# Attention column sums: the R matmuls in another place of TensorE's queue, and every second block's sums taken on ScalarE

## The chip, the cores and the metric

The kernel is one program on all 8 cores of one Trainium2 chip. Each core works on its own 4096 tokens and its own heads; nothing is exchanged between cores. The metric is the device time in microseconds of the slowest core, from one launch. The profile shows one execution, by its slowest core, core 2.

## The reference

One layer: attention and a feed-forward part with eight low-rank experts, each with layer norms and a residual. Only the attention's middle matters here:

```python
Q = Q.reshape(N, heads, L, dh)      # K and V the same; plain reshape
scores = jnp.einsum('neax,nebx->neab', Q * scale, K * scale)
A = jax.nn.softmax(scores, axis=2)              # over a, the query index
Out = jnp.einsum('neab,neax->neax', A, V)       # A is summed over b
```

The softmax runs over `a`, and the second product only sums `A` over `b`. So with e = exp(scores) two vectors are wanted for each head: the column sums c[b], the sum of e[a,b] over a, and r[a], the sum of e[a,b] / c[b] over b. `Out` is then V times r. With L = 8192 and dh = 64, a core has eight heads and computes 8192 x 8192 exponentials for each.

## The kernel before

The program has four blocks in order. Block A makes the layer norm and Q, K and V; Q and K stay in SBUF as `qt` and `kt`, two heads to a tile of 128 partitions, four pairs of heads. Block B computes r. Block C applies it and the output projection, block D is the feed-forward part. Every engine has its own queue, written out by hand; semaphores tie the queues together. The change touches block B alone.

Block B runs over K = 0 to 255: `p = K // 64` is the pair of heads, `k` the chunk of 128 key positions b. One K is called a step here. A step has these parts:

- **Fills**, TensorE L421 and L427. For each of eight pairs of slots (`s2`), four matmuls 64x512 write scores of 1024 query positions for head A and for head B, the two heads in the two halves of the array at once. `ps_sl` has three slots of 128x1024 in PSUM. The fill of one pair waits for the head-A exponential of the pair before it (`s_exp >= gsB - 2`).
- **Exponentials**, ScalarE L463, or L455 where `K % 8 == 0`: sixteen of 128x1024, head A and head B by turns, from PSUM into `eA` and `eB` (bf16, two buffers each, by the parity of K). L455 also gives the sum of each row (`accum_out`, eight partial sums into `caA`, `caB`). Before step K ScalarE waits for R(K-2) (`s_rmm`), which frees the buffer, and for lhsTall of K-2 (`s_lhs`).
- **Column sums**, VectorE. After the last exponential of K, it adds the eight partial sums (L479, L481) where `K % 8 == 0`; else it scans `eA` and `eB`, 128x8192 each, with a running sum (L484, L488). Then two reciprocals, a memset, and two small writes (L497, L500) put 1/c into `lhsTall`; the second one sets `s_lhs`.
- **R(K)**, TensorE L390 and L397, function `emit_R`: sixteen pairs of matmuls 128x512 with a stationary operand of 16 columns, of which one holds 1/c; they add this step's share of r into the bank `rps`, head A in partitions 0 to 15, head B in 32 to 47. R(K) needs all exponentials of K and `s_lhs` of K. At the end of a pair of heads (`K % 64 == 63`) VectorE waits for R(K) and copies `rps` out.

The order on TensorE is: first fill of K, R(K-2), the other seven fills of K; after the last step R(254) and R(255).

Of the kernel before, what the change touches and what calls it, by code (L numbers as in the profile page):

```python
# [22 lines left out]
NK = 256  # L23
# [6 lines left out]
def build_program():  # L30
# [48 lines left out]
    with ExitStack() as top:  # L79
# [53 lines left out]
        with ExitStack() as scqt:  # L133
# [215 lines left out]
            with ExitStack() as sc2:  # L349
# [26 lines left out]
                @blockB.tensor  # L376
                def _(tensor):
                    if "B" not in DBG_PHASES:
                        return
                    def emit_R(Kr):  # L380
                        if Kr < 0:
                            return
                        p, k = Kr // 64, Kr % 64
                        par = Kr % 2
                        W(tensor, "s_exp", (Kr + 1) * 16)
                        W(tensor, "s_lhs", Kr + 1)
                        if k == 0:
                            W(tensor, "s_rev", p)
                        for j in range(16):
                            mm = tensor.matmul(  # L390
                                rps[0:16, :], lhsT_ap(par, j, 0),
                                eA[:, par, j * 512:(j + 1) * 512],
                                start=(k == 0 and j == 0),
                                stop=(k == 63 and j == 15),
                                skip_group_check=True,
                                tile_position=(0, 0))
                            mm = tensor.matmul(  # L397
                                rps[32:48, :], lhsT_ap(par, j, 1),
                                eB[:, par, j * 512:(j + 1) * 512],
                                start=(k == 0 and j == 0),  # L400
                                stop=(k == 63 and j == 15),
                                skip_group_check=True,
                                tile_position=(0, 32))
                        I(mm, "s_rmm")

                    for K in range(NK):
                        p, k = K // 64, K % 64
                        for s2 in range(8):
                            if s2 == 1:
                                emit_R(K - 2)  # L410
                            gsA = K * 16 + 2 * s2
                            gsB = gsA + 1
                            slA = gsA % 3
                            slB = gsB % 3
                            W(tensor, "s_exp", gsB - 2)
                            lhsA = kt[0:64, p, k * 128:(k + 1) * 128]
                            lhsB = kt[64:128, p, k * 128:(k + 1) * 128]
                            mms = []
                            for half in range(2):
                                a0 = s2 * 1024 + half * 512  # L420
                                mms.append(tensor.matmul(  # L421
                                    ps_sl[:, slA,
                                          half * 512:(half + 1) * 512],
                                    lhsA, qt[0:64, p, a0:a0 + 512],
                                    start=True, stop=True,
                                    tile_position=(0, 0)))
                                mms.append(tensor.matmul(  # L427
                                    ps_sl[:, slB,
                                          half * 512:(half + 1) * 512],
                                    lhsB, qt[64:128, p, a0:a0 + 512],  # L430
                                    start=True, stop=True,
                                    tile_position=(64, 0)))
                            I(mms[2], "s_fill")
                            I(mms[3], "s_fill")
                    emit_R(NK - 2)
                    emit_R(NK - 1)

                @blockB.scalar
                def _(scalar):
                    if "B" not in DBG_PHASES:  # L440
                        return
                    for K in range(NK):
                        par = K % 2
                        W(scalar, "s_rmm", K - 1)
                        W(scalar, "s_lhs", K - 1)
                        for s in range(16):
                            gs = K * 16 + s
                            head = s % 2
                            s2 = s // 2
                            sl = gs % 3  # L450
                            W(scalar, "s_fill", gs + 1)
                            ebuf = eA if head == 0 else eB
                            cab = caA if head == 0 else caB
                            if K % 8 == 0:
                                I(scalar.activation(  # L455
                                    ebuf[:, par, s2 * 1024:(s2 + 1) * 1024],
                                    ps_sl[:, sl, :], AF.Exp,
                                    scale=float(2.0 ** -10),
                                    bias=epsb[:, 1:2],
                                    accum_out=cab[:, par, s2:s2 + 1]),  # L460
                                  "s_exp")
                            else:
                                I(scalar.activation(  # L463
                                    ebuf[:, par, s2 * 1024:(s2 + 1) * 1024],
                                    ps_sl[:, sl, :], AF.Exp,
                                    scale=float(2.0 ** -10),
                                    bias=epsb[:, 1:2]), "s_exp")

                @blockB.vector
                def _(vector):  # L470
                    if "B" not in DBG_PHASES:
                        return
                    for K in range(NK):
                        par = K % 2
                        W(vector, "s_exp", (K + 1) * 16)
                        W(vector, "s_rmm", K - 1)
                        v0 = cnt["s_dv"]
                        if K % 8 == 0:
                            I(vector.reduce_sum(cA[:, 0:1], caA[:, par, :],  # L479
                                                axis=AX.X), "s_dv")  # L480
                            I(vector.reduce_sum(cB[:, 0:1], caB[:, par, :],  # L481
                                                axis=AX.X), "s_dv")
                        else:
                            I(vector.tensor_scalar(  # L484
                                eA[:, par, :], eA[:, par, :],
                                1.0, 0.0, ALU.mult, ALU.add,
                                accum_out=cA[:, 0:1]), "s_dv")
                            I(vector.tensor_scalar(  # L488
                                eB[:, par, :], eB[:, par, :],
                                1.0, 0.0, ALU.mult, ALU.add,  # L490
                                accum_out=cB[:, 0:1]), "s_dv")
                        vector.wait_ge(sem("s_dv"), v0 + 2)
                        I(vector.reciprocal(icA[:, 0:1], cA[:, 0:1]), "s_dv")
                        I(vector.reciprocal(icB[:, 0:1], cB[:, 0:1]), "s_dv")
                        I(vector.memset(lhsTall[:, par, :], 0.0), "s_dv")
                        vector.wait_ge(sem("s_dv"), v0 + 5)
                        I(vector.tensor_scalar(lhsT_write_ap(par, 0),  # L497
                                               ones16[:, :], icA[:, 0:1],
                                               None, ALU.mult), "s_dv")
                        I(vector.tensor_scalar(lhsT_write_ap(par, 1),  # L500
                                               ones16[:, :], icB[:, 0:1],
                                               None, ALU.mult), "s_lhs")
                        if K % 64 == 63:
                            pp = K // 64
                            W(vector, "s_rmm", K + 1)
                            I(vector.tensor_scalar(
                                r_ev[0:16, pp * 512:(pp + 1) * 512],
                                rps[0:16, :], -1.0, None, ALU.add), "s_dv")
                            I(vector.tensor_scalar(
                                r_od[0:16, pp * 512:(pp + 1) * 512],  # L510
                                rps[32:48, :], -1.0, None, ALU.add),
                              "s_rev")
# [715 lines left out]
```

How the kernel before makes its waits and increments, by code:

```python
        def W(eng, name, v):  # L107
            if v > 0:
                eng.wait_ge(sem(name), v)
# [1 line left out]
        def I(instr, name, k=1):  # L111
            instr.then_inc(sem(name), k)
            cnt[name] += k
# [47 lines left out]
                @blockA.sync  # L161
                def _(sync):
                    for dst, src in [
                        (bq[:, :], bq_d), (bk[:, :], bk_d), (bv[:, :], bv_d),
                        (bo[:, :], bo_d), (wib[:, :], wib_d),
                        (wob[:, :], wob_d), (gb[:, :], gb_d),
                        (identf8[:, :], ident_d[0:8, 0:8]),
                        (epsb[:, :], epsc_d),
                    ]:
                        I(sync.dma_start(dst, src), "sA", 16)
                    if "A" not in DBG_PHASES:
                        sync.wait_ge(sem("sA"), cnt["sA"])
                        return
                    for gi in range(NCH):
                        W(sync, "s_xfree", gi - 1)
                        I(sync.dma_start(xb[:, gi % 2, :],
                                         x_d[gi * 128:(gi + 1) * 128, :]),
                          "sX%d" % (gi % 2), 16)
# [1 line left out]
                @blockA.gpsimd  # L180
# [15 lines left out]
                    ]  # L196
                    assert len(loads) == N_GPRE
                    for dst, src in loads:
                        I(gpsimd.dma_start(dst, src), "sG", 16)
                    if "A" not in DBG_PHASES:
                        gpsimd.wait_ge(sem("sG"), cnt["sG"])
                        return
                    for e in range(NB):
```

## Time and the profile before

| | us |
|---|---|
| median of 3 runs | 9051.24 (9051.23 to 9086.05) |
| the profiled execution's own time | 9053.95 |
| its span on core 2 | 9052.4 |
| spans of the 8 cores | 9029.4 to 9052.4 |
| TensorE matmuls busy | 5074.8 |
| VectorE busy | 5402.6 |
| ScalarE busy | 4396.9 |
| block B, first to last exponential on core 2 | 658.9 to 6764.7 |

The span runs from the first to the last instruction of the core; the execution's time is a little longer. Busy times are sums over instructions of an engine. Block B has two thirds of the span. The granted TensorE clock has two levels, 1.2 and 2.4 GHz; the records give it as 0.5 and 1.0, and its mean over core 2 is 0.687.

### The profile page before, as it was taken

Reading aid. Unit: us, or ns where it says so; the run is one execution under the profiler, and the core shown is the slowest. Engines: PE = TensorE matmul, PEld = TensorE weight load, DVE = VectorE, ACT = ScalarE, POOL = GpSimd, SP = SyncE. Lnnn points to the kernel's source line nnn. Section 1 sums busy time; section 2 is a strip of 40 time slices with the busy share of each in tenths; the row PEclk is TensorE's granted clock in tenths of the full one; section 3 lists DMA queues with packets and bytes.
Section 4 is the critical chain, followed back from the end, with each engine's and each line's share of the span. In section 5 each row is a group of like instructions: output and inputs, shape, how many; then the busy total and the mean of one; then the engine's idle time right before and its main releaser. Section 6 shows DMA issues by size and latency. Waiting matters only on the chain. (4 is left out here: it accounts for less than half of the span.)

```text
span 9052.4 us, 69885 instructions; the slowest of 8 cores (9029.4 to 9052.4 us)
## 1 busy us (share of the span) xinstructions
PE 5074.8 (56%) x24072; PEld 1527.3 (17%) x24072; DVE 5402.6 (60%) x4272; ACT 4396.9 (49%) x4868; POOL 151.2 (2%) x144
## 2 busy tenths in 40 slices
PE   4665555555555555555555555555552336677776
PEld 2221111111111111111111111111111112233322
DVE  4656676767676666767676766676764663322223
ACT  0017677777767676767676777777660000000000
POOL 0000000000000000000000000000000000000000
PEclk8776666666666666666666666666665667888888
DMA  3100000000000000000000000000004224644565
GB/s 71 42 28 0 1 1 1 0 1 0 1 1 0 1 1 0 1 1 0 1 1 0 1 1 0 1 1 0 1 0 106 69 78 65 92 62 61 72 77 75
DMA packets 348262, 206.26 MB, mean 23 GB/s; under 512 B 303840, under 2 KB 320224, under 8 KB 346864
## 3 DMA queue, kind: packets, MB, share of 16 engines
q0 software_dynamic: 273920, 92.70, 9.1%
q1 hardware_dynamic: 74000, 109.10, 4.1%
q8 instruction: 202, 3.31, 0.2%
q14 instruction: 140, 1.15, 0.0%
HBM read 235.75 MB, written 50.33 MB: 32 GB/s over the span
## 5 line engine op out<-in xcount | busy, mean ns | idle before, releaser
L421 PE MATMUL ps_sl<-qt,kt 64*128 64x512 bf16 x4096 | 1850.2, 547 | 2831.4 <-ACT eA L463 2443.1
L484 DVE TENSOR_SCALAR_CACHE_REDUCE eA<-eA 128x8192 bf16<-128x8192 bf16 x224 | 1945.7, 8686 | 1658.0 <-ACT eB L463 1658.0
L463 ACT ACTIVATE eA<-ps_sl,epsb 128x1024 bf16<-128x1024 f32 x1792 | 1998.7, 1115 | 1569.9 <-PE rps L397 1293.8
L463 ACT ACTIVATE eB<-ps_sl,epsb 128x1024 bf16<-128x1024 f32 x1792 | 1992.4, 1112 | 0.0
L488 DVE TENSOR_SCALAR_CACHE_REDUCE eB<-eB 128x8192 bf16<-128x8192 bf16 x224 | 1944.5, 8681 | 0.0
L427 PE MATMUL ps_sl<-qt,kt 64*128 64x512 bf16 x4096 | 1894.9, 559 | 0.0
L390 PE MATMUL rps<-eA,lhsTall 128*16 128x512 bf16 x4096 | 1407.5, 520 | 16.2 <-DVE lhsTall L500 16.2
L397 PE MATMUL rps<-eB,lhsTall 128*16 128x512 bf16 x4096 | 1407.3, 520 | 0.0
L421 PEld LDWEIGHTS ps_sl<-qt,kt 64*128 64x128 bf16 x4096 | 274.6, 98 | 4315.2 <-issue 4315.2
L1057 ACT ACTIVATE s4lv<-s4vr,epsb 128x1 f32<-128x1 f32 x32 | 9.4, 294 | 1324.8 <-DVE s4vr L1141 1324.8
L390 PEld LDWEIGHTS rps<-eA,lhsTall 128*16 128x16 bf16 x4096 | 451.0, 115 | 1039.5 <-issue 895.7
L1029 PE MATMUL ps_wi<-interT,wotb 128*128 128x512 bf16 x2048 | 498.3, 409 | 135.3 <-DMA wotb<-wot 125.6
L1012 PE MATMUL ps_wi<-h2t,wit_s 128*128 128x512 bf16 x2048 | 494.9, 385 | 14.0 <-DVE mxr L1101 14.0
L397 PEld LDWEIGHTS rps<-eB,lhsTall 128*16 128x16 bf16 x4096 | 453.1, 116 | 0.0
L1109 DVE TENSOR_SCALAR interT<-ps_wi,wib_s 128x512 bf16<-128x512 f32 x256 | 192.2, 751 | 375.9 <-PE ps_wi L1017 375.9
L1117 DVE TENSOR_SCALAR ft_sb<-ps_wi,wob_s 128x512 bf16<-128x512 f32 x64 | 48.1, 751 | 585.9 <-PE ps_wi L1029 585.9
L455 ACT ACTIVATE eA<-ps_sl,epsb 128x1024 bf16<-128x1024 f32 x256 | 285.2, 1114 | 208.9 <-PE rps L397 184.0
L455 ACT ACTIVATE eB<-ps_sl,epsb 128x1024 bf16<-128x1024 f32 x256 | 284.0, 1109 | 0.0
L1029 PEld LDWEIGHTS ps_wi<-interT,wotb 128*128 128x128 bf16 x2048 | 210.2, 104 | 421.7 <-issue 217.5
L297 ACT ACTIVATE st_lv<-st_vr,epsb 128x1 f32<-128x1 f32 x32 | 9.4, 294 | 553.0 <-DVE st_vr L239 553.0
L700 PE MATMUL ps_h<-identb,h2b 128*128 128x128 bf16 x256 | 32.4, 305 | 396.7 <-DVE h2b L826 396.7
L427 PEld LDWEIGHTS ps_sl<-qt,kt 64*128 64x128 bf16 x4096 | 253.1, 104 | 0.0
(123 smaller groups left out, 3036.9 us busy)
## 6 DMA issues: line engine op xcount, KB each, us to landing
wotb<-wot POOLq DMA_DIRECT2D x64, 1024.0 KB, 11.2
xb<-x SPq DMA_DIRECT2D x64, 512.0 KB, 4.0
x1buf<-x1b SPq DMA_DIRECT2D x32, 512.0 KB, 5.0
x1b<-x1buf SPq DMA_DIRECT2D x32, 512.0 KB, 4.2
y<-yb SPq DMA_DIRECT2D x32, 512.0 KB, 5.0
vsp<-vt_tmp POOLq DMA_DIRECT2D x64, 128.0 KB, 2.2
vt<-vsp SPq DMA_DIRECT2D x8, 1024.0 KB, 6.1
wit_s<-wit POOLq DMA_DIRECT2D x1, 8192.0 KB, 69.1
```

The costliest lines, as they stand in the source:

```text
L390: mm = tensor.matmul(rps[0:16, :], lhsT_ap(par, j, 0), eA[:, par, j * 512:(j + 1) * 512], start=(k == 0 and j == 0), stop=(k == 63 and j = ...
L397: mm = tensor.matmul(rps[32:48, :], lhsT_ap(par, j, 1), eB[:, par, j * 512:(j + 1) * 512], start=(k == 0 and j == 0), stop=(k == 63 and j ...
L421: mms.append(tensor.matmul(ps_sl[:, slA, half * 512:(half + 1) * 512], lhsA, qt[0:64, p, a0:a0 + 512], start=True, stop=True, tile_positio ...
L427: mms.append(tensor.matmul(ps_sl[:, slB, half * 512:(half + 1) * 512], lhsB, qt[64:128, p, a0:a0 + 512], start=True, stop=True, tile_posit ...
L455: I(scalar.activation(ebuf[:, par, s2 * 1024:(s2 + 1) * 1024], ps_sl[:, sl, :], AF.Exp, scale=float(2.0 ** -10), bias=epsb[:, 1:2], accum_ ...
L463: I(scalar.activation(ebuf[:, par, s2 * 1024:(s2 + 1) * 1024], ps_sl[:, sl, :], AF.Exp, scale=float(2.0 ** -10), bias=epsb[:, 1:2]), "s_exp")
L484: I(vector.tensor_scalar(eA[:, par, :], eA[:, par, :], 1.0, 0.0, ALU.mult, ALU.add, accum_out=cA[:, 0:1]), "s_dv")
L488: I(vector.tensor_scalar(eB[:, par, :], eB[:, par, :], 1.0, 0.0, ALU.mult, ALU.add, accum_out=cB[:, 0:1]), "s_dv")
L1012: tensor.matmul(ps_wi[:, fc % 2, :], wit[:, ci, fc * 128:(fc + 1) * 128], h2t4[:, par, ci, :], start=(ci == 0), stop=False)
L1029: mm = tensor.matmul(ps_wi[:, co % 2, :], wotb[:, co % 2, fc, :], interT[:, fc, :], start=(fc == 0), stop=(fc == FC - 1))
L1109: I(vector.tensor_scalar(interT[:, fc, :], ps_wi[:, fc % 2, :], wib[:, fc:fc + 1], 0.0, ALU.add, ALU.max), "s4_ie")
L1117: I(vector.tensor_scalar(ft_sb[:, e % 2, co, :], ps_wi[:, co % 2, :], wob[:, co:co + 1], None, ALU.add), "s4_fe")
```

## The change

The R matmuls change place: `emit_R(K - 1)` stands behind all eight fills of K, where before `emit_R(K - 2)` stood behind the first fill of K. The condition for row sums on ScalarE becomes `K % 2 == 0` on both engines, so that VectorE scans only the odd steps. The flag `skip_group_check=True` of the R matmuls goes. Waits, buffers and semaphores stay as they are; their values follow the calls.

```diff
--- before.py
+++ after.py
@@ -392,22 +392,18 @@
                                 eA[:, par, j * 512:(j + 1) * 512],
                                 start=(k == 0 and j == 0),
                                 stop=(k == 63 and j == 15),
-                                skip_group_check=True,
                                 tile_position=(0, 0))
                             mm = tensor.matmul(
                                 rps[32:48, :], lhsT_ap(par, j, 1),
                                 eB[:, par, j * 512:(j + 1) * 512],
                                 start=(k == 0 and j == 0),
                                 stop=(k == 63 and j == 15),
-                                skip_group_check=True,
                                 tile_position=(0, 32))
                         I(mm, "s_rmm")
 
                     for K in range(NK):
                         p, k = K // 64, K % 64
                         for s2 in range(8):
-                            if s2 == 1:
-                                emit_R(K - 2)
                             gsA = K * 16 + 2 * s2
                             gsB = gsA + 1
                             slA = gsA % 3
@@ -432,7 +428,7 @@
                                     tile_position=(64, 0)))
                             I(mms[2], "s_fill")
                             I(mms[3], "s_fill")
-                    emit_R(NK - 2)
+                        emit_R(K - 1)
                     emit_R(NK - 1)
 
                 @blockB.scalar
@@ -451,7 +447,7 @@
                             W(scalar, "s_fill", gs + 1)
                             ebuf = eA if head == 0 else eB
                             cab = caA if head == 0 else caB
-                            if K % 8 == 0:
+                            if K % 2 == 0:
                                 I(scalar.activation(
                                     ebuf[:, par, s2 * 1024:(s2 + 1) * 1024],
                                     ps_sl[:, sl, :], AF.Exp,
@@ -475,7 +471,7 @@
                         W(vector, "s_exp", (K + 1) * 16)
                         W(vector, "s_rmm", K - 1)
                         v0 = cnt["s_dv"]
-                        if K % 8 == 0:
+                        if K % 2 == 0:
                             I(vector.reduce_sum(cA[:, 0:1], caA[:, par, :],
                                                 axis=AX.X), "s_dv")
                             I(vector.reduce_sum(cB[:, 0:1], caB[:, par, :],
```

## Rows read from the trace of the kernel before

**Rows 1.** The page's 40 equal slices: busy tenths of ScalarE, TensorE's clock in tenths.
```profile
ACT  0017677777767676767676777777660000000000
...
PEclk8776666666666666666666666666665667888888
```

**Rows 2.** The page's groups: busy us, mean ns of one; idle before, releaser.
```profile
L463 ACT ACTIVATE eA<-ps_sl,epsb 128x1024 bf16<-128x1024 f32 x1792 | 1998.7, 1115 | 1569.9 <-PE rps L397 1293.8
...
L455 ACT ACTIVATE eA<-ps_sl,epsb 128x1024 bf16<-128x1024 f32 x256 | 285.2, 1114 | 208.9 <-PE rps L397 184.0
```

**Rows 3.** Times of L463: ns, first and last start; idle before it, times.
```profile
L463 ACT ACTIVATE eA<-ps_sl,epsb x1792: 1113/1113/1132, 678.5 to 6763.7; 128x1024 bf16<-128x1024 f32 x200
...
  PE rps L397: 1293.8, 223
```

**Rows 4.** Timeline of one plain step, K = 99: start us, duration us.
```profile
3014.87 0.59 PE L390 MATMUL rps<-eA,lhsTall 128*16 128x512 bf16 x1
...
3019.99 0.38 PE L390 MATMUL rps<-eA,lhsTall 128*16 128x512 bf16 x1
...
3020.59 1.11 ACT L463 ACTIVATE eA<-ps_sl,epsb 128x1024 bf16<-128x1024 f32 x1 [5.83 <-PE rps L397]
...
3021.84 0.37 PE L421 MATMUL ps_sl<-qt,kt 64*128 64x512 bf16 x1 [1.47 <-ACT eA L463]
...
3022.06 0.37 PE L421 MATMUL ps_sl<-qt,kt 64*128 64x512 bf16 x1
...
3024.59 1.13 ACT L463 ACTIVATE eA<-ps_sl,epsb 128x1024 bf16<-128x1024 f32 x1
...
3026.97 1.11 ACT L463 ACTIVATE eA<-ps_sl,epsb 128x1024 bf16<-128x1024 f32 x1 [0.25 <-PE ps_sl L427]
...
3036.42 1.11 ACT L463 ACTIVATE eA<-ps_sl,epsb 128x1024 bf16<-128x1024 f32 x1 [0.24 <-PE ps_sl L427]
3037.43 1.11 ACT L463 ACTIVATE eB<-ps_sl,epsb 128x1024 bf16<-128x1024 f32 x1
```

**Rows 5.** Timeline of VectorE there: the sums of K = 98.
```profile
3014.95 8.69 DVE L484 TENSOR_SCALAR_CACHE_REDUCE eA<-eA 128x8192 bf16<-128x8192 bf16 x1 [4.99 <-ACT eB L463]
...
3033.36 0.26 DVE L500 TENSOR_SCALAR lhsTall<-ones_s,icB 128x16 bf16<-128x16 bf16 x1
```

**Rows 6.** Two windows of it: busy us (times) by engine; PEclk is the clock.
```profile
3014.86:3018.72 3.86, 3.86 (x22) 1.30 (x22) 3.77 (x1) 0.00 (x0) 0.00 (x0) 0.50 0.00 0
3018.72:3025.55 6.83, 2.87 (x24) 0.82 (x20) 6.83 (x3) 4.96 (x5) 0.00 (x0) 1.00 0.00 0
```

**Rows 7.** Timeline at the end of block B: R(254) and R(255).
```profile
6762.94 0.63 PE L421 MATMUL ps_sl<-qt,kt 64*128 64x512 bf16 x1
...
6763.53 0.59 PE L390 MATMUL rps<-eA,lhsTall 128*16 128x512 bf16 x1
...
6763.67 1.11 ACT L463 ACTIVATE eA<-ps_sl,epsb 128x1024 bf16<-128x1024 f32 x1 [0.24 <-PE ps_sl L427]
...
6768.25 0.38 PE L390 MATMUL rps<-eA,lhsTall 128*16 128x512 bf16 x1
...
6784.80 0.59 PE L390 MATMUL rps<-eA,lhsTall 128*16 128x512 bf16 x1 [16.17 <-DVE lhsTall L500]
...
6790.80 0.38 PE L390 MATMUL rps<-eA,lhsTall 128*16 128x512 bf16 x1
```

**Rows 8.** Timeline of ScalarE in one summing step, K = 96.
```profile
2948.80 1.11 ACT L455 ACTIVATE eA<-ps_sl,epsb 128x1024 bf16<-128x1024 f32 x1 [5.93 <-PE rps L397]
2949.81 0.19 ACT L455 ACTIVATION_READ_ACCUMULATOR eA<-ps_sl,epsb 128x1 f32 x1
...
2953.16 1.12 ACT L455 ACTIVATE eA<-ps_sl,epsb 128x1024 bf16<-128x1024 f32 x1
...
2955.63 1.11 ACT L455 ACTIVATE eA<-ps_sl,epsb 128x1024 bf16<-128x1024 f32 x1 [0.15 <-PE ps_sl L427]
...
2965.44 1.11 ACT L455 ACTIVATE eA<-ps_sl,epsb 128x1024 bf16<-128x1024 f32 x1 [0.15 <-PE ps_sl L427]
```

## The prediction

> **What bounds the kernel now.** I read the page's slices first, then the times of one line, then the order of events in single steps of block B. The slices [rows 1] show block B as the long flat middle, from the third to the 31st of 40 slices, with ScalarE at six or seven tenths and a granted clock of TensorE between its levels. The page's groups [rows 2] say what fills it: exponentials of 128x1024 at about 1.115 us each, 3584 on L463 and 512 on L455. The times of L463 [rows 3] give the length of a step. The first head-A exponential of K = 1 starts at 678.5 and that of the last pair of K = 255 at 6763.7. Inside one step the same distance (first to last pair) is 3036.42 - 3020.59 = 15.83 us [rows 4], so 254 steps take 6085.2 - 15.8 = 6069.4 us, 23.895 us each. Of this ScalarE stands idle waiting for the last R matmul (L397) 223 times, 1293.8 us, 5.8 us each time [rows 3].
>
> The order of events in a step [rows 4] says why. R(K-2) starts at 3014.87, its sixteenth pair of matmuls at 3019.99, and ScalarE, idle for 5.83 us, starts at 3020.59. R stands behind the first fill on TensorE, the first fill waits for the last head-A exponential of the step before, and ScalarE may not begin step K before R(K-2) has freed the exponentials' buffer. So R lies entirely on the path. After it the eight pairs go at 2.00 us while the clock is at 2.4 GHz (20.59 to 24.59, two pairs) and at 2.36 us when it is at 1.2 GHz (26.97 to 36.42, four pairs): at the low clock a fill is longer than the head-B exponential beside it, and ScalarE loses 0.24 us a pair. VectorE's two scans are not the limit: they start at 3014.95 and the last write of lhsTall starts at 3033.36 [rows 5], well before the step's end.
>
> **The clock.** TensorE is at 1.2 GHz when R starts and stays there for 3.86 us with 22 matmuls back to back (the last two of the fill and ten pairs of R, so 0.42 us from one pair to the next), and at 2.4 GHz for the next 6.83 us [rows 6]; then, with a short fill every 2 us, it is low again for the rest of the step. R buys the fast clock for its own second half and for two fills.
>
> **Part 1, R(K-1) behind all fills of K, instead of R(K-2) behind its first one.** R(0) to R(253) are moved; matmuls and weight loads stay the same in number. The new order stands once in this trace, at the end of block B, where R(254) already follows the fills of K = 255 [rows 7]. The last fill's third matmul starts at 6762.94, R at 6763.53, and the last head-A exponential at 6763.67, so R runs beside the last two exponentials. I write down the distance from the start of that exponential (A7) to the first one of the next step (A0). R starts 0.14 before A7 [rows 7]. First to last of its pairs is 5.12 [rows 4]. Then comes the first fill of the next step; its slot is free, since its wait is for A7. The step from R's last pair to it shows nowhere in this order: at least 0.22, the spacing of matmuls at the fast clock (3021.84 to 3022.06, [rows 4]), and at most 0.59, the opposite change at the low clock (6762.94 to 6763.53, [rows 7]). I take 0.30, near the low end, because the clock is high there. From the fill's first matmul to A0: 0.22 to its third, which lasts 0.37 [rows 4], and 0.10 of handoff, as from the third's end at 6763.57 to 6763.67 [rows 7]: 0.69. Sum: -0.14 + 5.12 + 0.30 + 0.69 = 5.97 us.
>
> In the kernel before, this distance is 23.895 less the mean first-to-last distance. That is 15.83 for a plain step and, for a step with the sums on ScalarE (which I call a summing step), 2965.44 - 2948.80 = 16.64 [rows 8]; one in eight: 15.93. So 7.96, and the move saves 1.99 us a step. It isn't the whole 5.8: A7 and B7 hide 2.1 of R, the old first fill was hidden and the new one's 0.69 is not.
>
> The weight change at that step has a rule. The Trainium skill, "TensorE: Matmul & The Clock Gate", section "The mechanism" under packing, says that a weight load overlaps running matmuls only where their row groups differ. R uses all 128 rows, so by the rule a fill's load of about 0.1 us would stand bare behind it and the step would be some 0.32, 5 us more in all. No row here shows that step; the sum doesn't use it.
>
> **Part 2, sums on ScalarE in every second K instead of every eighth.** The summing steps among K = 1 to 254 rise from 31 to 127, by 96. Each exponential there is followed by an accumulator read of about 0.2 us [rows 8]. It costs less than its sixteen reads, because at the low clock it lies in the 0.24 us that ScalarE would wait for the fill. Two of its pairs take 2.18 us at the fast clock and the others 2.46 [rows 8]. First to last pair is 16.64 against 15.83, 0.81 a step: 96 x 0.81 = 78 us slower. VectorE loses two scans of 8.69 us in 96 steps, about 1670 us of its work. That is worth nothing by itself, as it was hidden, but it gives the cover that part 1 needs. R(K-1) now waits for lhsTall of K-1 at the end of K instead of one fill into K+1. After a plain K-1 (always odd) it is ready 3033.36 + 0.26 - 3014.76 = 18.9 us after the end of its last exponential, where 3014.76 is A0's start less its idle time [rows 4, 5]. R wants it after the new gap, 5.97 - 2.12 = 3.85 (2.12 from A7's start to B7's end: 3036.42, 3037.43 + 1.11), and the seven pairs of a summing K, 16.64, less 0.14: at 20.35 us. So 1.4 us of slack. Were K plain too, 0.6 would be left; if it fell short, the fills queued behind R on TensorE would be late, and ScalarE with them. After a summing K-1 the wait is for a few small instructions.
>
> **Part 3, the dropped group-check flag**: no instruction's shape or count comes from it; nothing.
>
> **Sum.** Plain step 15.83 + 5.97 = 21.80; summing step 16.64 + 5.97 = 22.61; 127 of each: mean 22.205 against 23.895, 1.69 x 254 = 429 us less. By parts: 254 x 1.99 - 78 = 427. The first step, the last R and the other blocks are unchanged. The profiled execution, 9053.95 (span 9052.4), would become 8624.7; against the median of the runs, 9051.24, it is 8622.
>
> **The rivals.** *The clock rises later or earlier in R.* The step isn't as even as before: plain and summing steps differ by 0.8 us, so R meets the clock's rise elsewhere. Three R of this trace differ in just this: first to last pair 5.12 in the step shown, 4.72 for R(254), 6.00 for R(255) [rows 4, 7]. Later: +0.88 x 254 = +224, 8846 us. Earlier: -0.40 x 254 = -102, 8520. The clock then also ends earlier or later against the fills, one pair of 0.36 us the other way, so both are outer values. The page on TensorE named above says, under "What's actually happening", that the place of the rise changes from run to run; the three R agree that it isn't fixed.
>
> *Slower: the clock doesn't rise at all.* The fills alone never raise it in the low part of a step. If R's run were broken up, R would take 15 times 0.42 = 6.3 us (1.2 more), the bare fill 1.11 in place of 0.69 (0.42 more; from its third matmul's start it is 0.73 at the low clock, 6762.94 to 6763.67, and 0.38 lies ahead of that), and the two fast pairs 0.36 or, with sums, 0.28 more each (2.46 less 2.18, [rows 8]; 0.64 in the mean): 2.3 us a step, 580 us, 9202 in all. It decides from 1.69 us a step. For it: the change makes the busy stretch depend on lhsTall. Against: R now has a fill directly ahead and one directly behind, and R(254) in that place got the fast clock [rows 7]. The same page's table "Why this matters for your kernels" warns that pauses between bursts bring the low clock; that stays true of the fills here, before and after.
>
> *The move gives nothing,* because ScalarE waits for the fill behind R as it waited for R; then only the reads count: 9051 + 78 = 9129. R(254), with A7 starting 0.14 us into it [rows 7], speaks against it.
>
> *R waits for lhsTall.* Each us beyond the slack costs 127 us; 1 us gives 8749. The slack of 1.4 us speaks against it.
>
> **How the numbers follow.** Forecast 0.75; clock later 0.12; clock earlier 0.05; R waits 0.03; clock never 0.03; nothing from the move 0.02. The time is the forecast's, 8622. Its own bounds, the step of 0.22 to 0.59, give 8602 to 8696. With the earlier clock below, and a part of the later one and a short wait above, the range is 8515 to 8740. Half a per cent, 45 us, is about what a measurement of this kernel can tell from no change. Faster 0.94, same 0.01, slower 0.05.
>
> **What would show it.** In the profile after: the distance between first exponentials of two neighbouring steps sums to about 44.4 us; ScalarE's idle time before A0 is about 3.85 us and put down to the fill's matmul, not R's; A7 starts within 0.2 us of R's start; no idle time of TensorE before R for VectorE; 1024 accumulator reads a head instead of 256; 128 scans a head instead of 224; R first to last near 5.1. Wrong would be: R of 6 us in most steps, an idle time before R, or pairs of more than 2.46 us in summing steps.

## The result and the profile after

The changed kernel takes 8623.7 us in the median of eight executions, against 8622 forecast. The kernel before, run beside it, took 9070.4; the ratio is 0.951, with a 95% interval of 0.949 to 0.953. In some executions the cores of one die or of both show a lower granted clock and take some per cent longer, so times given here as medians are of the other executions, only one of which is left of e9_split_sums_warm, and the profile of e7_changed_warm is of such a longer one. The profiled execution took 8629.9 us, its slowest core 7. These are lines of its page, which answer to [rows 1] and [rows 2]. The groups give busy us, mean ns of one, and the idle time before it with what ended it.

```profile
DVE  4663444444444444444444444444436653322233
ACT  0007777777777777777777787777730000000000
...
PEclk8886666666666666666666666666665658988877
...
L480 DVE TENSOR_SCALAR_CACHE_REDUCE eA<-eA 128x8192 bf16<-128x8192 bf16 x128 | 1111.8, 8686 | 2456.6 <-ACT eB L459 2456.6
...
L451 ACT ACTIVATE eA<-ps_sl,epsb 128x1024 bf16<-128x1024 f32 x1024 | 1142.2, 1115 | 671.0 <-PE ps_sl L423 658.6
L459 ACT ACTIVATE eA<-ps_sl,epsb 128x1024 bf16<-128x1024 f32 x1024 | 1143.1, 1116 | 530.0 <-PE ps_sl L423 530.0
```

VectorE's scans are 128 for head A and as many for head B, where they were 224 each; one takes 8.69 us as in [rows 5]. The releaser of ScalarE's idle time has changed: before it was R (L397), now it is the matmul of a fill (L423 is the fill's head B here). The exponentials themselves take 1.115 us as before.

The times of L459 on core 7 (columns as in [rows 3]) give the length of a step: 6330.6 - 679.3 less 15.83, over 254, is 22.187 us. The forecast was 22.205, before it was 23.895.

```profile
L459 ACT ACTIVATE eA<-ps_sl,epsb x1024: 1114/1114/1132, 679.3 to 6330.6; 128x1024 bf16<-128x1024 f32 x171
...
  PE ps_sl L423: 530.0, 770
```

The first of two neighbouring transitions on core 7, timeline: R behind the last fill of a plain step, the last head-A exponential A7, R's last pair, the first fill of the next step, A0.

```profile
3002.49 0.59 PE L390 MATMUL rps<-eA,lhsTall 128*16 128x512 bf16 x1
...
3002.63 1.11 ACT L459 ACTIVATE eA<-ps_sl,epsb 128x1024 bf16<-128x1024 f32 x1 [0.24 <-PE ps_sl L423]
...
3008.25 0.38 PE L390 MATMUL rps<-eA,lhsTall 128*16 128x512 bf16 x1
...
3008.57 0.39 PE L417 MATMUL ps_sl<-qt,kt 64*128 64x512 bf16 x1
...
3009.27 1.11 ACT L451 ACTIVATE eA<-ps_sl,epsb 128x1024 bf16<-128x1024 f32 x1 [4.52 <-PE ps_sl L423]
```

This is the sum of the prediction, term by term, in one transition: R 0.14 ahead of A7, R's first to last pair 5.76 (5.12 was taken), from there to the fill 0.32 (0.30), from the fill to A0 0.70 (0.69). ScalarE's idle time is 4.52, forecast 3.85. The next transition on the same core, behind a summing step:

```profile
3025.79 0.59 PE L390 MATMUL rps<-eA,lhsTall 128*16 128x512 bf16 x1
...
3025.92 1.11 ACT L451 ACTIVATE eA<-ps_sl,epsb 128x1024 bf16<-128x1024 f32 x1 [0.15 <-PE ps_sl L423]
...
3030.15 0.38 PE L390 MATMUL rps<-eA,lhsTall 128*16 128x512 bf16 x1
...
3030.47 0.39 PE L417 MATMUL ps_sl<-qt,kt 64*128 64x512 bf16 x1
...
3031.17 1.11 ACT L459 ACTIVATE eA<-ps_sl,epsb 128x1024 bf16<-128x1024 f32 x1 [2.94 <-PE ps_sl L423]
```

Here R takes 4.36 and the idle time is 2.94; the step from R to the fill is again 0.32. From A7 to A0 it is 5.25 in one and 6.64 in the other, 5.95 in the mean (5.97 forecast). A third pair of rows from the same core shows that this goes on by turns:

```profile
3047.00 1.11 ACT L459 ACTIVATE eA<-ps_sl,epsb 128x1024 bf16<-128x1024 f32 x1 [0.24 <-PE ps_sl L423]
...
3053.64 1.11 ACT L451 ACTIVATE eA<-ps_sl,epsb 128x1024 bf16<-128x1024 f32 x1 [4.52 <-PE ps_sl L423]
```

Core 2, same execution, has the other pattern: the long transition comes behind the summing step.

```profile
3005.06 1.11 ACT L451 ACTIVATE eA<-ps_sl,epsb 128x1024 bf16<-128x1024 f32 x1 [3.39 <-PE ps_sl L423]
...
3021.71 1.11 ACT L451 ACTIVATE eA<-ps_sl,epsb 128x1024 bf16<-128x1024 f32 x1 [0.15 <-PE ps_sl L423]
...
3028.08 1.11 ACT L459 ACTIVATE eA<-ps_sl,epsb 128x1024 bf16<-128x1024 f32 x1 [4.07 <-PE ps_sl L423]
```

Its idle times are 3.39 and 4.07; the step shown is 23.02 us, and the one behind it 21.36, 44.38 together. On core 7 the two make 44.37 (3009.27 to 3053.64). Cores 6 and 7 have the first pattern and cores 0 to 5 the second. So no core has the even transition of the prediction; its mean is there, 5.91 to 5.95 us on all eight.

The granted clock over two steps of core 7, in windows cut where it changes (busy us and times by engine; the clock is the number after POOL):

```profile
3007.62:3014.45 6.83, 2.77 (x22) 0.67 (x18) 6.83 (x3) 5.18 (x9) 0.00 (x0) 1.00 0.00 0
3014.45:3028.10 13.65, 7.43 (x32) 1.63 (x34) 8.89 (x7) 12.89 (x24) 0.00 (x0) 0.50 0.00 1
3028.10:3034.93 6.83, 4.07 (x34) 1.24 (x30) 1.34 (x7) 3.89 (x6) 0.00 (x0) 1.00 0.00 0
3034.93:3052.00 17.07, 10.37 (x48) 2.54 (x48) 2.69 (x1) 12.97 (x13) 0.00 (x0) 0.50 0.00 1
```

One high stretch of 6.83 us belongs to each step, as before. The low stretch behind it was 17.07 us in the kernel before; here it is 13.65 and 17.07 by turns.

### The profile page after: what moved, and what is told of

Read it like the earlier page. It is cut to its first block and busy times, and to the rows that moved or that the text cites. A ratio compares the mean times of both kernels' runs of the same rounds, so it can differ in the third digit from the quotient of the medians.

```text
span 8628.3 us, 71229 instructions; the slowest of 8 cores (8600.0 to 8628.3 us)
## 1 busy us (share of the span) xinstructions
PE 4962.3 (58%) x24072; PEld 1517.7 (18%) x24072; DVE 3764.3 (44%) x4080; ACT 4540.8 (53%) x6404; POOL 151.2 (2%) x144
## 5 line engine op out<-in xcount | busy, mean ns | idle before, releaser
L417 PE MATMUL ps_sl<-qt,kt 64*128 64x512 bf16 x4096 | 1746.7, 519 | 2539.8 <-ACT eA L451 1318.0
L480 DVE TENSOR_SCALAR_CACHE_REDUCE eA<-eA 128x8192 bf16<-128x8192 bf16 x128 | 1111.8, 8686 | 2456.6 <-ACT eB L459 2456.6
L423 PE MATMUL ps_sl<-qt,kt 64*128 64x512 bf16 x4096 | 1786.1, 530 | 0.0
L459 ACT ACTIVATE eA<-ps_sl,epsb 128x1024 bf16<-128x1024 f32 x1024 | 1143.1, 1116 | 530.0 <-PE ps_sl L423 530.0
L390 PE MATMUL rps<-eA,lhsTall 128*16 128x512 bf16 x4096 | 1393.2, 516 | 15.1 <-DVE lhsTall L496 15.1
L459 ACT ACTIVATE eB<-ps_sl,epsb 128x1024 bf16<-128x1024 f32 x1024 | 1139.9, 1113 | 0.0
L484 DVE TENSOR_SCALAR_CACHE_REDUCE eB<-eB 128x8192 bf16<-128x8192 bf16 x128 | 1111.1, 8681 | 0.0
L417 PEld LDWEIGHTS ps_sl<-qt,kt 64*128 64x128 bf16 x4096 | 267.4, 97 | 3909.0 <-issue 3909.0
L475 DVE TENSOR_REDUCE cA<-caA 128x1 f32<-128x8 f32 x128 | 20.5, 160 | 622.1 <-ACT eB L451 622.1
```

The source lines that it names most:

```text
L390: mm = tensor.matmul(rps[0:16, :], lhsT_ap(par, j, 0), eA[:, par, j * 512:(j + 1) * 512], start=(k == 0 and j == 0), stop=(k == 63 and j = ...
L417: mms.append(tensor.matmul(ps_sl[:, slA, half * 512:(half + 1) * 512], lhsA, qt[0:64, p, a0:a0 + 512], start=True, stop=True, tile_positio ...
L423: mms.append(tensor.matmul(ps_sl[:, slB, half * 512:(half + 1) * 512], lhsB, qt[64:128, p, a0:a0 + 512], start=True, stop=True, tile_posit ...
L459: I(scalar.activation(ebuf[:, par, s2 * 1024:(s2 + 1) * 1024], ps_sl[:, sl, :], AF.Exp, scale=float(2.0 ** -10), bias=epsb[:, 1:2]), "s_exp")
L480: I(vector.tensor_scalar(eA[:, par, :], eA[:, par, :], 1.0, 0.0, ALU.mult, ALU.add, accum_out=cA[:, 0:1]), "s_dv")
L484: I(vector.tensor_scalar(eB[:, par, :], eB[:, par, :], 1.0, 0.0, ALU.mult, ALU.add, accum_out=cB[:, 0:1]), "s_dv")
```

## The experiments

**Part 1 alone (e1_move_only)**: both conditions back to one step in eight.

```diff
-if K % 2 == 0:      # exponentials and column sums
+if K % 8 == 0:
```

> Part 1 alone: R(K-1) behind the fills of K as in the changed kernel, sums on ScalarE where K % 8 == 0 as before. Theory A (the step is the sum of its parts): plain steps 21.80 us, 31 summing steps 22.61, mean 21.90 against 23.895, 507 us less than before, some 8545 (78 below the changed kernel), and the 0.6 us of slack of R against the scan is just enough. Theory B (the steps fall into step with the clock's rises and falls, so that a step's length is set by where R meets the rise): steps of unequal length from about 20.9 to 22.6, mean near 21.76, some 8510. Rival C (R waits for lhsTall after two plain steps and the fills behind it are late): an idle time of TensorE before R put down to VectorE, and at 1 us or more in most steps the gain over the changed kernel is gone.

Measured: 8515.7 us in the median, ratio 0.941 (0.934 to 0.949). This is 108 us less than the changed kernel. The two weren't run side by side, but the steps say the same: 22.187 less 21.76, times 254, is 108 us. Core 0, who waited for lhsTall (total us, times), and the exponentials' first and last start:

```profile
L390 PE MATMUL rps<-eA,lhsTall x4096: 379/417/634, 705.8 to 6259.2; 128*16 128x512 bf16 x196
...
  DVE lhsTall L496: 30.1, 65
```

```profile
L459 ACT ACTIVATE eA<-ps_sl,epsb x1792: 1114/1114/1133, 689.4 to 6232.1; 128x1024 bf16<-128x1024 f32 x200
```

The step is (6232.1 - 689.4 - 15.83) / 254 = 21.76 us; theory B said 21.76, theory A 21.90. R does wait for VectorE, in 64 steps besides the last R (whose 16.2 us are the scan itself), but 30.1 - 16.2 = 13.9 us over 64 waits is 0.2 us each. Rival C is out at this size. Steps of 20.92, 21.37 and 22.58 us stand side by side. The clock's low stretch is 13.65 us in 158 of the steps and 17.07 in the others.

**Part 2 alone (e2_sums_only)**: the kernel before with the sums of every second step on ScalarE.

```diff
-if K % 8 == 0:
+if K % 2 == 0:
```

> Part 2 alone: R(K-2) behind the first fill of K as before, sums on ScalarE where K % 2 == 0. Theory A: the reads cost 0.81 us in each of 96 more steps, 78 us, so 0.9% slower than before. Theory B: a summing step is longer and the plain one behind it shorter by the same, the two together as long as the high and the low stretch of the clock in two steps (2 x 23.9), so within 0.1% of before. VectorE's lower load changes nothing in either.

Measured: 9053.8 us in the median, beside 9057.9 of the kernel before; ratio 0.998 (0.995 to 1.001). 96 more summing steps cost nothing that can be seen. A0 of three neighbouring steps on core 0:

```profile
3020.26 1.11 ACT L463 ACTIVATE eA<-ps_sl,epsb 128x1024 bf16<-128x1024 f32 x1 [5.25 <-PE rps L397]
...
3043.85 1.11 ACT L455 ACTIVATE eA<-ps_sl,epsb 128x1024 bf16<-128x1024 f32 x1 [5.63 <-PE rps L397]
...
3068.05 1.11 ACT L463 ACTIVATE eA<-ps_sl,epsb 128x1024 bf16<-128x1024 f32 x1 [5.25 <-PE rps L397]
```

The plain step is 23.59 and the summing one 24.20, together 47.79: two high and two low stretches of the clock, 2 x (6.83 + 17.07) = 47.80, which is what the clock's records of this core show in all steps but one. The kernel before has the same stretches (the high one of 6.83 us is in [rows 6]) and its mean step is as long as the two. The reads do lengthen the pairs: the mean distance from A0 to A7 is 16.25 us, where it was 15.94. But R's first to last pair is 4.78 in the mean, where it was 5.12, because R meets the rise of the clock sooner, and so the step stays as it was. This is theory B. The 78 us of the prediction are there in the pairs and are given back by R.

**All sums on ScalarE in the changed order (e3_all_sums)**

```diff
-if K % 2 == 0:
+if True:
```

> The changed kernel with the sums on ScalarE in every step, no scan on VectorE at all. Theory A: every step 22.61 us, 254 x 0.405 = 103 us slower than the changed kernel, some 8725. Theory B: mean near 22.53, some 8710, steps unequal. If lhsTall were what holds R anywhere in the changed kernel, this one would be faster than it.

Measured: 8691.6 us, ratio 0.958 (0.953 to 0.963); the mean step is 22.52 on core 2, with steps from 21.7 to 23.3. That is B's mean; it is 18 us below B's total and 33 below A's. The changed kernel isn't held by lhsTall anywhere: its TensorE waits for lhsTall once, before the last R (15.1 us on core 7), and taking the scan away altogether makes it 68 us slower.

**No sums on ScalarE (e4_no_sums)**

```diff
-if K % 2 == 0:
+if K < 0:
```

> The changed order of R with no sums on ScalarE at all: VectorE scans every step. It takes away the cover of part 2 to the last. Theory A: plain steps of 21.80 us and 0.6 us of slack left for the scan, so 254 x 0.405 = 103 us less than the changed kernel, some 8520. Theory B (settling with the clock): steps of about 20.9, 21.4 and 22.6 by turns, mean near 21.63, some 8480; TensorE waits some 0.4 us for lhsTall before an R in the shorter ones and this costs nothing, because a later R meets the rise of the clock sooner. Rival C: the wait for lhsTall falls on the steps, mean above 22.2, and the sums on ScalarE were needed.

Measured: 8522.8 us in the median (8495.3 the lowest), ratio 0.938 (0.932 to 0.944). Core 4, waits for lhsTall and the exponentials' first and last start (K = 0 included):

```profile
  DVE lhsTall L496: 47.8, 88
```

```profile
L459 ACT ACTIVATE eA<-ps_sl,epsb x2048: 1114/1115/1135, 658.3 to 6204.6; 128x1024 bf16<-128x1024 f32 x187
```

(6204.6 - 658.3 - 15.86) / 255 = 21.69 us a step, near B's 21.63 and 0.11 below A. The 87 waits before the last are 31.6 us, 0.36 each. Against e1_move_only (21.75 over the same steps, its first included) they cost nothing that can be seen; a late R meets the clock's rise sooner (4.80 us in the mean from its first to its last pair). At the three borders between pairs of heads a step takes 26.3 us, because VectorE copies `rps` out before it can begin the next scan. In e1_move_only, with a summing step there, none is above 23.1, so the borders eat up part of what this one would have gained on it.

**The clock held high in both orders (e8_all_sums_warm, e10_before_all_sums_warm)**: three matmuls whose result nobody reads stand behind each of seven fills, so TensorE has work in every pair. All sums are on ScalarE in both, so only R's place differs. The added matmuls change no output.

```diff
+dps = e2(nc.psum_tensor("dps", [128, 512], F32))
...
 I(mms[3], "s_fill")
+for _d in range([3, 3, 3, 3, 3, 3, 3, 0][s2]):
+    tensor.matmul(dps[:, :], kt[:, p, k * 128:(k + 1) * 128],
+                  qt[:, p, 0:512], start=True, stop=True)
```

(In e10_before_all_sums_warm the list is `[0, 3, 3, 3, 3, 3, 3, 3]` and R is `emit_R(K - 2)` behind the first fill.)

> e3_all_sums (sums on ScalarE in every step) with the same added matmuls as e7_changed_warm. No scan, so no wait for VectorE: every step 7 x 2.18 + 4.0 = 19.3 us against 22.52 of e3_all_sums, 820 us less than it, some 7870. If e7_changed_warm shows the wait for lhsTall, this one is faster than it by some 100 us, although without the added matmuls all sums on ScalarE were slower.

> The order of before, R(K-2) behind the first fill, with the sums on ScalarE in every step and three matmuls that nobody reads behind the fills 1 to 7, so that the clock stays high: the counterpart of e8_all_sums_warm (step 19.30), with only the place of R different. It measures the move without the clock. First to last pair 15.3; then the fill waits 1.45 for A7 and its sum, takes 0.5, R 3.2 and the handoff 0.6: 5.8, step 21.1. So the move is worth 1.8 us a step at a steady clock, against 1.99 in the sum of the prediction; some 8320 in all.

Measured, one execution each: 7864.9 us and 8346.2 us. ScalarE's first and last start and its idle time, core 0, first e8_all_sums_warm:

```profile
L456 ACT ACTIVATE eA<-ps_sl,epsb x2048: 1112/1154/1272, 657.9 to 5593.5; 128x1024 bf16<-128x1024 f32 x187
...
  PE ps_sl L424: 479.8, 257
```

Then e10_before_all_sums_warm:

```profile
L460 ACT ACTIVATE eA<-ps_sl,epsb x2048: 1112/1141/1265, 658.5 to 6069.7; 128x1024 bf16<-128x1024 f32 x187
...
  PE rps L398: 870.0, 254
  PE ps_sl L428: 70.3, 62
```

Between A0 of K = 0 and A7 of K = 255 stand 255 steps and 15.3 us: 19.3 us a step in the one and 21.2 in the other. Both sums of parts, 19.3 and 21.1, hold to 0.1 us once the clock is nearly still: it is at 2.4 GHz for over 99% of block B in the one and for 96 to 97% in the other, and R's first to last pair is 3.24 us in both, in every step of core 0. Moving R is worth 1.9 us a step there, 481 us in all, of which 460 are idle time of ScalarE before head-A exponentials (870.0 + 70.3 less 479.8). From A7 to A0 alone it is 1.77 us; the rest is in the pairs, from the short low stretches that only e10_before_all_sums_warm has.

**The changed kernel with the clock held high (e7_changed_warm)**: the same added matmuls in the changed kernel.

> The changed kernel with three matmuls that nobody reads behind each of the fills 0 to 6, so that the clock stays high. It takes the clock out of the step: ScalarE's first to last pair falls to 7 x 2.00 = 14.0 in a plain step and 7 x 2.18 = 15.3 in a summing one, R to 15 x 0.215 = 3.2, and the distance from A7 to the next A0 to some 4.0. Then the scan is no longer covered: lhsTall of a plain K-1 is ready 18.9 us after its last exponential, R wants it after 1.9 + 15.3 - 0.2 = 17.0. Expected: plain step 18.0, summing step 19.3 + 2 of waiting for VectorE, mean 19.7, 630 us less than the changed kernel, some 7990, with an idle time of TensorE of about 2 us before every second R. If the clock isn't what sets the step's length, it stays near 22.2.

Measured: 8181 us in the median, 8179 in the lowest, ratio 0.905 (0.895 to 0.915); 191 us above the forecast. The wait for VectorE came, and it came with something else. The profiled execution took 8330.7 us, but its excess lies behind block B (2427 to 2439 us on cores 2 to 5, 2271 to 2281 on the others). In block B the mean step is 20.46 to 20.48 us on all eight cores, against 19.7 forecast, and 255 times this difference is the 191 us and a little more. Core 3, end of a summing step behind a plain one:

```profile
4027.86 1.20 ACT L456 ACTIVATE eA<-ps_sl,epsb 128x1024 bf16<-128x1024 f32 x1
...
4029.68 0.59 PE L391 MATMUL rps<-eA,lhsTall 128*16 128x512 bf16 x1 [1.97 <-DVE lhsTall L501]
...
4032.61 0.38 PE L391 MATMUL rps<-eA,lhsTall 128*16 128x512 bf16 x1
...
4034.34 0.38 PE L391 MATMUL rps<-eA,lhsTall 128*16 128x512 bf16 x1
...
4035.36 1.11 ACT L464 ACTIVATE eA<-ps_sl,epsb 128x1024 bf16<-128x1024 f32 x1 [5.11 <-PE ps_sl L424]
```

Three windows over it (busy us and times by engine; the clock is the number after POOL):

```profile
4024.00:4029.20 5.20, 2.05 (x12) 0.50 (x11) 4.93 (x6) 5.20 (x11) 0.00 (x0) 1.00 0.00 2
4029.20:4032.60 3.40, 2.92 (x14) 1.01 (x16) 1.68 (x9) 1.05 (x2) 0.00 (x0) 0.50 0.03 5
4032.60:4036.00 3.40, 3.40 (x27) 1.09 (x23) 0.00 (x0) 0.64 (x1) 0.00 (x0) 1.00 0.00 0
```

TensorE stands idle for 1.97 us before R, and R finds the clock at 1.2 GHz, which it keeps for 3.4 us; it takes 4.66 instead of 3.2, and the step is 22.8 instead of the 21.3 forecast (the plain one is 18.1, forecast 18.0). What I had not priced is the clock's fall in the idle time. The same execution shows a third level of the clock in other stretches, core 0, one window of 200 us:

```profile
3000.00:3200.00 200.00, 160.06 (x840) 42.97 (x839) 94.92 (x79) 166.31 (x235) 0.00 (x0) 0.81 0.00 1
```

Here it is granted at 0.81, and matmuls of R follow at 0.26 us instead of 0.22. This level has 47% of block B on core 0 and 13% on core 3, and the mean step is the same on both; so in block B of this kernel it costs nothing that can be seen. Behind block B it does: cores 2 to 5 have it there for 1200 us or more, the others not at all.

**R spread over the fills (e5_spread)**: sums on ScalarE in every step, and R(K-1) cut into pieces behind the fills 1 to 7 of K.

```diff
+RC = [0, 0, 3, 6, 8, 10, 12, 14, 16]     # first pair of R behind each fill
...
 I(mms[3], "s_fill")
-emit_R(K - 1)                            # behind all fills
+emit_R(K - 1, RC[s2], RC[s2 + 1])        # pairs j0 to j1 - 1; the waits at
+                                         # j0 == 0, s_rmm at j1 == 16
```

> A version meant to be better. Sums on ScalarE in every step, so that 1/c of K-1 is ready about 2 us after the last exponential of K-1; the sixteen pairs of R(K-1) are spread behind the fills 1 to 7 of K, as 3, 3, 2, 2, 2, 2, 2. TensorE is idle for 1.4 us in every pair of slots and two pairs of R take 0.85 at the low clock, so R leaves the path, if the weight changes between fill and R cost no more than some 0.2 us each way. Expected: a step of eight pairs at 2.46 us if the clock stays low, 19.7, some 8000 in all; at 2.18 us if it stays high, 17.5, some 7440. If fills wait for R instead: a pair of slots above 2.5 us and little gain over the changed kernel.

Measured: 7667.5 us, ratio 0.844 (0.839 to 0.849). Core 6, low clock: three pairs of R, one fill, the next piece of R.

```profile
3009.94 0.59 PE L391 MATMUL rps<-eA,lhsTall 128*16 128x512 bf16 x1
...
3010.08 1.11 ACT L454 ACTIVATE eA<-ps_sl,epsb 128x1024 bf16<-128x1024 f32 x1 [0.15 <-PE ps_sl L426]
...
3010.76 0.63 PE L391 MATMUL rps<-eA,lhsTall 128*16 128x512 bf16 x1
...
3011.43 0.58 PE L420 MATMUL ps_sl<-qt,kt 64*128 64x512 bf16 x1
...
3012.39 0.59 PE L391 MATMUL rps<-eA,lhsTall 128*16 128x512 bf16 x1
...
3012.53 1.11 ACT L454 ACTIVATE eA<-ps_sl,epsb 128x1024 bf16<-128x1024 f32 x1 [0.15 <-PE ps_sl L426]
```

The next head-A exponential comes 2.45 us after the last, as in a summing step without R between its fills [rows 8] (2.46 there): R costs nothing. The page:

```profile
ACT  0005999999999999999999999999100000000000
...
PEclk9787777777777777777777777777665588888888
```

ScalarE is busy in nine tenths, and the step is 18.48 us, between the two bounds 17.5 and 19.7, since the clock is high for about half of the time. Against e3_all_sums, with the same sums, the step is 4.0 us shorter. Even with the clock low throughout it would be 2.8 shorter (22.52 less the 19.7 of the expectation, an estimate); the rest comes with the clock, which is high for 54% of block B here and for 30% there.

**The same with the clock held high (e6_spread_warm)**: one to four added matmuls behind each fill, by `[4, 1, 1, 2, 2, 2, 2, 2]`.

> e5_spread with matmuls added that nobody reads (128x512 into a spare bank: 4 behind fill 0, 1 behind fills 1 and 2, 2 behind the others), so that TensorE is busy for about 1.2 us of every 2.2 in all of block B and the clock, once it is at 2.4 GHz, has no cause to fall. In e5_spread a step was 18.48 us in the mean with pairs of 2.18 and 2.46 us mixed. Theory B (what is left is the clock): all pairs 2.18, step 17.45, 255 x 1.03 = 260 us less than e5_spread, some 7400. If the added matmuls get in the way of the fills instead, the step is longer than 18.5.

Measured: 7509.8 us, ratio 0.828 (0.824 to 0.832). The step is 17.53 us (17.45 forecast), 0.95 less than in e5_spread (242 us in all). The total came out only 158 us lower; the rest lies outside block B, where the code is the same. On the slowest core, 3, the part behind block B took 2368 us, 88 more than on the slowest of e5_spread. The extra time goes with the 0.81 level: cores 2 to 5 have it for some 900 us behind block B and take 2349 to 2368 us there, the others have none of it and take 2261 to 2274. Ahead of block B it is the other way round: cores 0, 1, 6 and 7 have it for 370 to 410 us and take 699 to 706 us, the others 655 to 657. What brings this level on is open.

**Head B's sums in pieces on VectorE (e9_split_sums_warm)**: from e6_spread_warm, with ScalarE's sums for head A only, R behind the fills 2 to 7, and the added matmuls by `[4, 4, 1, 1, 1, 1, 2, 2]`.

```diff
-RC = [0, 0, 3, 6, 8, 10, 12, 14, 16]
+RC = [0, 0, 0, 3, 6, 9, 12, 14, 16]
...
+for c in range(8):
+    W(vector, "s_exp", K * 16 + 2 * c + 2)
+    I(vector.tensor_scalar(eB[:, par, c * 1024:(c + 1) * 1024],
+                           eB[:, par, c * 1024:(c + 1) * 1024],
+                           1.0, 0.0, ALU.mult, ALU.add,
+                           accum_out=caB[:, par, c:c + 1]), "s_dv")
```

> A version meant to be better still, from e6_spread_warm: head B's sums go to VectorE, which adds up each 128x1024 piece while the exponentials run (about 1.1 us each, estimated as an eighth of the scan's 8.69), head A's stay on ScalarE. R(K-1) begins behind fill 2, since 1/c comes some 3 us after the last exponential. ScalarE's pair is 1.10 + 1.005 = 2.10 instead of 2.18, step 16.8: 255 x 0.65 = 160 us less than e6_spread_warm, some 7240. If 1/c comes later than fill 2's end, the fills behind R are late and the gain is smaller.

Measured: 7263.7 us in one execution, 0.80 of the 9051.5 that was the lowest of the kernel before beside it. No interval can be given for it. Its new group on core 5:

```profile
L481 DVE TENSOR_SCALAR_CACHE_REDUCE eB<-eB 128x1024 bf16<-128x1024 bf16 x2048 | 2492.3, 1218 | 1390.4 <-ACT eB L467 1390.0
```

A piece of 128x1024 takes 1.22 us instead of 1.1, which is still covered. The step is 16.8 us in 234 of 255, as forecast, and 16.9 in the mean, since a few take over 20 us. This is the fastest version seen; ScalarE's exponentials alone are 16 x 1.0 us of it.

## Why the prediction was right

- *What bounds the kernel.* Right: R on the path with ScalarE idle, and pairs of 2.00 or 2.36 us by the clock. e5_spread shows it from the other side: with R off the path, and the clock high for longer by it, 4 us a step go.
- *R's new place.* The terms -0.14, 0.30 and 0.69 were measured at -0.14, 0.32 and 0.70. The estimate for the middle one by the Trainium skill ("TensorE: Matmul & The Clock Gate", "The mechanism") was 0.32, since there a weight load overlaps running matmuls only where their row groups differ. The size agrees with the trace; the rule doesn't hold throughout in it. R's own loads share all 128 rows with the matmuls that run, and yet its pairs follow at 0.22 us with a load of 0.09 in between (core 7, 3007.82 to 3008.04). What costs the 0.10 more between R and a fill is not shown.
- *R's own time.* I took 5.12 for every step. Hardly a step has it: 5.76 and 4.36 on core 7, with a mean of 5.06. The rivals "clock later" and "clock earlier" are both there, by turns, and cancel. My bounds for them, 6.00 and 4.72, were taken as alternatives to each other, which they aren't, and 4.36 lies below the lower one. This is the weak step of the prediction: R was a constant, but the runs show its mean at 5.12, 4.78, 4.85 or 5.06 us, by what else stands in the step.
- *The two parts.* Both were mis-sized, through R, and against each other. The move alone was put at 505 us (254 x 1.99) and is worth 542 (9057.9 less 8515.7). The sums were put at 78 us; they cost 108 in the new order (8623.7 less 8515.7) and 0 in the old one. The 0.81 us of a summing step isn't what was wrong: from A0 to A7 the sums add 0.29 to 0.31 us to the mean step in both orders, 74 to 79 us in all (table below). The rest is R. In the new order it is 0.21 us longer with the sums (against that, the waits of e1_move_only, 0.07 in the mean, are gone), in the old order 0.34 shorter. That the two errors, 37 and 30 us, cancel in the total is luck.
- *The cover that the sums would give.* It wasn't needed. I had put the slack at 0.6 us with plain steps on both sides; the runs show R late by 0.2 to 0.4 us in some steps, because a short step comes sooner than the mean one, and no loss by it. A wait costs time only once the rest is faster: in e7_changed_warm it is near 2 us and costs more than itself, since the clock falls in it.
- *The dropped flag.* Matmuls and weight loads are 24072 each before and after. No run tries the flag alone, so that it costs and gives nothing isn't shown by itself.
- *The rivals that ended otherwise.* The clock did rise in every R: on every core all 256 begin at 1.2 GHz and end at 2.4. "The move gives nothing" is refuted by e1_move_only, 542 us faster, and by R's row 0.14 us ahead of A7.

Means over the 254 steps from K = 1 to 254, worked out from the starts in the traces, us:

| | core | A0 to A7 | A7 to next A0 | of it R, first to last pair | step |
|---|---|---|---|---|---|
| before | 2 | 15.94 | 7.96 | 5.12 | 23.90 |
| e2_sums_only | 0 | 16.25 | 7.65 | 4.78 | 23.90 |
| e1_move_only | 0 | 15.96 | 5.80 | 4.85 | 21.76 |
| changed | 7 | 16.25 | 5.94 | 5.06 | 22.19 |
| forecast for it | | 16.24 | 5.97 | 5.12 | 22.21 |

The clock's records give the last column once more. Each step has one high stretch of 6.83 us, and a low one of 13.65 or 17.07, so 20.48 or 23.90 together. In the first two rows the short one comes once in all of block B, in e1_move_only in 158 of the 254 steps and in the changed kernel in 127; the weighted means are 23.90, 21.77 and 22.19.

That the steps fall in with the clock is shown by e2_sums_only (a pair of steps as long as the clock's two rounds, at no cost) and by e8_all_sums_warm and e10_before_all_sums_warm, where the sum of parts holds to 0.1 us as soon as the clock hardly changes. What decides which of the two patterns a core takes was not tried. The expectations' means by theory B (21.76, 22.53, 21.63 us) came out within 0.07 us, but no working is written down for them, so the share of short and long low stretches can't be forecast from what is shown here.

## What to carry to other kernels

Work that needs nothing from the engine it blocks belongs into that engine's waits, in pieces as small as the waits: moving R whole saved 1.7 to 2.1 us a step, cutting it into pieces for each wait saved 5.4, part of it through the clock, which was then high for longer. Where the clock rises and falls once in each round of a loop, a small cost can vanish (78 us forecast, 0 found) or grow (108), so such a part is tried alone and not taken from the whole's result. To see the parts themselves, hold the clock still with work that nobody reads, in both versions, and compare those. Of a change with two parts, run both alone: here one part gave all the gain and the other took a fifth of it back.

## What the runs showed of the hardware

- In the kernel before, a step of 23.9 us is one high stretch of 6.83 us and a low one of 17.07. In the changed kernel the high stretches are also 6.83, with 13.65 and 17.07 by turns between them, and two steps are 44.37 us, the sum of the four (44.38).
- Cores of one execution, with the same program, settle in different patterns (2.94 and 4.52 us of idle time, or 3.39 and 4.07) with the same mean step.
- With matmuls added to seven of the eight pairs, the granted clock is 1.00 for over 99% of block B on every core of e8_all_sums_warm, but 0.81 for 13 to 47% of it by core in e7_changed_warm (matmuls of R 0.26 us apart). There the mean step doesn't depend on that share (20.46 to 20.48 us on all cores), while the blocks behind block B take 2427 us or more with it and 2281 or less without.
- In e7_changed_warm the clock fell to 1.2 GHz near the end of a pause of 1.97 us before R and stayed there for 3.4 us, so that R took 4.66 us where it takes 3.24 at the high clock.
- ScalarE's exponentials at the full rate: 1.115 us each in the records, and 1.00 to 1.09 from one start to the next; an accumulator read of 0.2 us adds only 0.09 to that distance.
